# Linear attention of layer 0: the unread 2-byte matmuls inside its groups removed, the eight at its head kept

## The chip, the cores and the metric

One core of one Trainium2 chip runs the whole program. The metric is the device time of one execution in microseconds (us); lower is better. The engines are TensorE (PE in the profile, with its weight loads as PEld), VectorE (DVE), ScalarE (ACT), GpSimd (POOL) and the DMA queues.

## The reference

The program computes a small language-model tower: token embedding with neighbours, then four layers, each of an attention and a mixture of experts, on a stream h of 4 sequences x 512 tokens x 64 channels. The change touches only the first attention, which is linear attention with 8 heads of 32 key channels:

```
def _L0_attn_ref(x, Wks, Wqs, Wvs, Wo):
    keys = jnp.einsum('bsd,hdk->hbsk', x, Wks)
    queries = jnp.einsum('bsd,hdk->hbsk', x, Wqs)
    values = jnp.einsum('bsd,hde->hbse', x, Wvs)
    keys = jax.nn.elu(keys) + 1.0
    queries = jax.nn.elu(queries) + 1.0
    ...
    kv = jnp.einsum('hbsk,hbsd->hbsdk', keys, values)
    kv_cum = jnp.cumsum(kv, axis=2)
    numerator = jnp.einsum('hbsdk,hbsk->hbsd', kv_cum, queries)
    denominator = jnp.einsum('hbsk,hbsk->hbs', jnp.cumsum(keys, axis=2), queries)
    node = numerator / (denominator[..., None] + EPS)
    out = jnp.einsum('hbsd,hde->bse', node, Wo)
h = h + _L0_attn_ref(_layernorm(h, axis=-1), L0_attn_Wks, L0_attn_Wqs, L0_attn_Wvs, L0_attn_Wo)
```

## The kernel before

Everything is one program in stages, one after the other; the stage of this document is `linear_attention` (line 779), called once from `l0_attn` (line 2083) with G = 8 groups. A group g is four heads of one sequence (sequence g // 2, heads 4 * (g % 2) to 4 * (g % 2) + 3), and its two pairs of heads are p = 0 and 1. The 512 tokens of a sequence are cut into TB = 4 chunks of 128. Matrix operands are float32; one such matmul in the program stands as two in the trace.

For each group TensorE runs these steps, in this order (`diagonals` to `outs`, lines 841 to 899):

- `diagonals(g)`, L850: keys times queries inside each chunk, 16 matmuls over 32 rows each, into two banks per pair. VectorE then multiplies them by the causal mask into AT (L998, one instruction per pair, signal `masked`).
- `turn(g)`, L857: three transposes of key chunks. ScalarE copies them to KK (L942, `keys_ready`).
- `outs(g - 1, 0)` and `outs(g - 1, 1)`, L897: the result of the group before, CT, times the folded weights VO. VectorE divides by the denominator (L974, L976, L981, `heads_normed`) and GpSimd adds the heads to H (L1018).
- `state(g)`, L864: the running key-value sums. ScalarE copies them to SS (L944, `state_ready`).
- `within(g)`, L875: masked scores times values, 16 matmuls, into banks 6 and 7.
- `proj(g + 2)`, L838: keys and queries of the group after next. ScalarE takes them through Relu and Exp (L932, L935) and VectorE finishes them into QT and KT (L964, `qk_ready`).
- `across(g)`, L884: the sums of earlier chunks times the queries. ScalarE copies the result to CT (L949, `ctx_ready`).

Banks 0 to 5 of PSUM are three slots of two banks that go round over the steps in the order of `units`; before a step writes, `slot` waits until the step three places back has been read. By that rule `turn(g)` waits for `qk_ready` of group g + 1, and `outs(g - 1, p)` waits for `masked` of pair p of group g.

`unread(n, a)` (line 887) issues n matmuls of the bfloat16 identity, 128 x 128, on itself as 128 x 512, into bank a. Nothing reads what they write. They stand at three places: eight at the head of the stage (line 906); two in each `outs`, after `slot` and ahead of the wait for `ctx_ready` (line 893); and two in each group between `state` and `within` (line 916).

On VectorE a group also holds `draw` (L786, L788), work for a later stage. The queue of SyncE loads late weights in the first 8 us of the stage. The stage ends with a barrier of all engines.

Of the kernel before, what the change touches and what calls it, by code (L numbers as in the profile page):

```python
# [40 lines left out]
class Tally:  # L41
# [10 lines left out]
    def at(self, k):  # L52
        return self.i * self.per + (self.start + k) if self.per else self.start + k


def bc(ap, axis, n):

    shape = list(ap.shape)
    shape.insert(axis, n)
    return ap.unsqueeze(axis).to_broadcast(shape)  # L60
# [48 lines left out]
def _program(nc, T, out, ctx):  # L109
# [43 lines left out]
    C, a = {}, 0  # L153
# [625 lines left out]
    def linear_attention(G, batch, project, vo_src, vo_of, values, dst, eps):  # L779
# [39 lines left out]
        with nc.Block() as block:  # L819
# [6 lines left out]
            def _(eng):  # L826
                def slot(u):
                    n = number[u]
                    if n >= 3:
                        signal, value = freed(units[n - 3])  # L830
                        eng.wait_ge(signal.sem, value)
                    return bank(u)

                def proj(g):
                    a = slot(("P", g, 0))
                    for j in range(2):
                        for out, w, x in project(g, 0, j):
                            ins = nc.tensor.matmul(PS[out, a + j, :], w, x, start=True, stop=True, skip_group_check=True)  # L838
                    ins.then_inc(proj_done.sem, 1)

                def diagonals(g):
                    eng.wait_ge(qk_ready.sem, at(qk_ready, 2 * g + 1))
                    for p in range(2):
                        slot(("D", g, p))
                    for c in range(TB):
                        for p in range(2):
                            a = bank(("D", g, p))
                            for j in range(2):
                                h = rr(2 * p + j)
                                ins = nc.tensor.matmul(PS[:, a + j, chunk(c)], KT[h, g % 3, chunk(c)], QT[h, g % 3, chunk(c)], start=True, stop=True, skip_group_check=True)  # L850
                            if c == TB - 1:
                                ins.then_inc(diag_done.sem, 1)

                def turn(g):
                    a = slot(("T", g, 0))
                    for c in range(TB - 1):
                        ins = nc.tensor.transpose(PS[:, a, chunk(c)], KT[:, g % 3, chunk(c)], ident)  # L857
                    ins.then_inc(turned.sem, 1)

                def state(g):  # L860
                    a = bank(("T", g, 0)) + 1
                    eng.wait_ge(keys_ready.sem, at(keys_ready, g))
                    for c in range(TB - 1):
                        ins = nc.tensor.matmul(PS[:, a, c * D:(TB - 1) * D].rearrange("p (n d) -> p n d", d=D), KK[:, c, :], bc(XO[:, batch(g, 0) * TB + c, :], 1, TB - 1 - c),  # L864
                                               start=c == 0, stop=True, skip_group_check=True)
                    ins.then_inc(state_done.sem, 1)

                def within(g):
                    for p in range(2):
                        eng.wait_ge(masked.sem, at(masked, 2 * g + p))  # L870
                        if g >= 1:
                            eng.wait_ge(ctx_ready.sem, at(ctx_ready, 2 * (g - 1) + p))
                        for c in range(TB):
                            for j in range(2):
                                nc.tensor.matmul(PS[half(j), 6 + p, chunk(c)], XO[:, batch(g, j) * TB + c, :], AT[:, p, j, c, :],  # L875
                                                 start=c == 0, stop=c == 0, skip_group_check=True)

                def across(g):
                    eng.wait_ge(state_ready.sem, at(state_ready, g))
                    for p in range(2):  # L880
                        for c in range(1, TB):
                            for j in range(2):
                                h = rr(2 * p + j)
                                ins = nc.tensor.matmul(PS[half(j), 6 + p, chunk(c)], SS[h, c - 1, :], QT[h, g % 3, chunk(c)], start=False, stop=True, skip_group_check=True)  # L884
                        ins.then_inc(mixed.sem, 1)

                def unread(n, a):
                    for _ in range(n):
                        nc.tensor.matmul(PS[:, a, :], identh[:], bc(identh[:], 1, TB), start=True, stop=True, skip_group_check=True)

                def outs(g, p):
                    a = slot(("O", g, p))
                    unread(2, a)
                    eng.wait_ge(ctx_ready.sem, at(ctx_ready, 2 * g + p))
                    for c in range(TB):
                        for j in range(2):
                            ins = nc.tensor.matmul(PS[:, a + j, c * (D + 1):(c + 1) * (D + 1)], CT[half(j), p, chunk(c)], VO[half(j), vo_of(g, p), :],  # L897
                                                   start=True, stop=True, skip_group_check=True)
                    ins.then_inc(heads_out.sem, 1)
# [9 lines left out]
                for g in range(G):  # L909
                    diagonals(g)  # L910
                    turn(g)
                    if g >= 1:
                        outs(g - 1, 0)
                        outs(g - 1, 1)
                    state(g)
                    unread(2, 6)
                    within(g)
                    if g + 2 < G:
                        proj(g + 2)
                    across(g)  # L920
                outs(G - 1, 0)
                outs(G - 1, 1)

# [2129 lines left out]
```

## Time and profile before

| | us |
|---|---|
| median of 3 runs | 1049.62 (1047.46 to 1064.9) |
| profiled execution, its own time | 1049.9 |
| its span, first to last instruction | 1048.0 |
| mean granted clock of TensorE over the span | 0.925 of 2.4 GHz |
| the stage of the change, first `diagonals` to the last VectorE instruction | 122.9 to 221.7 |

Times within a trace count from the span's start. In a row of the page or of a view by lines, the engine, the line, the operation and out<-in stand first, then busy time or duration, and then the idle time of the engine just before with what ended it. The granted clock is 1.00 at 2.4 GHz and 0.50 at 1.2 GHz; TensorE has only these two levels in this trace, so a value between them is a mean over a stretch that has both. A row of busy time by stretches reads: the stretch A:B and its length, then the busy time of PE, PEld, DVE, ACT and POOL with the number of instructions, then TensorE's granted clock, the share of the DMA engines and GB/s.

### The profile page before, as it was taken

To read this page: it belongs to the slowest core of one execution; us is meant where nothing else is said; L and a number is where in the kernel's file an instruction comes from. 1 tells how busy PE (TensorE), PEld (TensorE's weight loads), DVE (VectorE), ACT (ScalarE), POOL (GpSimd) and SP (SyncE) were. 2 spreads that over 40 slices of the span, in tenths; PEclk is the share of its full clock that TensorE was granted. 3 is DMA by queue.
4 is the path that set the end of the run, shared out by engine and by line. 5 is a ranking of instruction groups with operands and counts; after the bars stand their busy time and mean duration, and the time that the engine had idled before them with its cause. 6 is when DMAs were issued, how large, how long until landed. Compare 5 with 4: busy or idle time off the path is not lost. (4 is left out here: it accounts for less than half of the span.)

```text
span 1048.0 us, 17078 instructions
## 1 busy us (share of the span) xinstructions
PE 904.0 (86%) x6611; PEld 454.4 (43%) x6611; DVE 649.8 (62%) x1734; ACT 368.5 (35%) x645; POOL 223.3 (21%) x291
## 2 busy tenths in 40 slices
PE   1988788979997865997898879999998799979998
PEld 0577566652323334762455333333333344443333
DVE  4977556567675264997467554555653555677665
ACT  0113533234543332223435314444444023443222
POOL 2600022215336031430230320121223402100000
PEclk9998899899999986998998968999999688989999
DMA  9300300000000001000000000000000000000000
GB/s 305 84 1 2 98 2 2 2 2 1 1 1 1 1 1 43 2 2 1 1 1 1 1 1 1 1 1 1 2 1 1 1 1 1 1 2 1 5 6 11
DMA packets 11477, 15.41 MB, mean 15 GB/s; under 512 B 8268, under 2 KB 9324, under 8 KB 10398
## 3 DMA queue, kind: packets, MB, share of 16 engines
q1 hardware_dynamic: 9976, 13.20, 4.2%
q10 hardware_dynamic: 1418, 1.09, 0.4%
q8 instruction: 54, 0.88, 0.4%
q14 instruction: 29, 0.24, 0.1%
HBM read 13.76 MB, written 0.52 MB: 14 GB/s over the span
## 5 line engine op out<-in xcount | busy, mean ns | idle before, releaser
L622 DVE TENSOR_REDUCE mx<-PS 128x2 f32<-128x1024 f32 (+3 forms) x104 | 109.6, 1095 | 103.8 <-PE PS L440 96.9
L582 ACT ACTIVATE arena<-PS 128x1024 f32<-128x1024 f32 (+3 forms) x104 | 91.0, 923 | 130.3 <-PE PS L470 130.3
L1217 DVE TENSOR_TENSOR arena<-arena,PS 128x512 f32<-128x512 f32 (+1 forms) x144 | 97.0, 684 | 45.0 <-ACT arena L1192 40.8
L1121 PE MATMUL PS<-XT,late 64*128 64x512 f32 (+1 forms) x288 | 101.9, 650 | 11.0 <-PEq L2502 6.6
L485 PE MATMUL PS<-arena 128*64 128x512 f32 (+3 forms) x416 | 99.8, 569 | 0.5 <-DVE arena L683 0.4
L465 PE MATMUL PS<-arena 32*128 32x512 f32 (+4 forms) x416 | 78.6, 622 | 9.7 <-ACT arena L559 7.4
L1192 ACT ACTIVATE arena<-PS,f_b_sb 128x512 f32<-128x512 f32 x96 | 61.8, 685 | 63.2 <-PE PS L1121 61.8
L1153 PE MATMUL PS<-arena,late 128*64 128x512 f32 (+1 forms) x288 | 81.6, 617 | 0.9 <-DVE arena L1217 0.7
L440 PE MATMUL PS<-arena 32*128 32x512 f32 (+4 forms) x416 | 72.8, 643 | 5.8 <-DVE arena L615 2.6
L1121 PEld LDWEIGHTS PS<-XT,late 64*128 64x128 f32 (+1 forms) x288 | 28.2, 183 | 62.5 <-ACT arena L1192 41.5
L1192 ACT ACTIVATE arena<-PS 114x512 f32<-114x512 f32 x48 | 27.4, 596 | 67.6 <-PE PS L1123 66.9
L1209 DVE TENSOR_TENSOR arena<-arena,PS 114x512 f32<-114x512 f32 x48 | 32.8, 683 | 28.8 <-ACT arena L1192 28.7
L727 POOL TENSOR_TENSOR H<-H,arena 128x256 f32<-128x256 f32 x30 | 21.8, 725 | 134.9 <-DVE arena L654 132.7
L465 PEld LDWEIGHTS PS<-arena 32*128 32x128 f32 (+1 forms) x416 | 29.9, 195 | 40.8 <-issue 18.5
L485 PEld LDWEIGHTS PS<-arena 128*64 128x64 f32 x416 | 22.1, 136 | 56.8 <-issue 38.9
L440 PEld LDWEIGHTS PS<-arena 32*128 32x128 f32 (+1 forms) x416 | 24.5, 203 | 49.6 <-issue 25.7
L2034 PE MATMUL PS<-identh 128*128 128x512 bf16 x91 | 31.6, 501 | 14.4 <-PEq L402 5.5
L1562 PE MATMUL PS<-late 128*128 128x128 fp8e5 x512 | 35.8, 235 | 7.2 <-DVE late L1471 7.2
L1123 PE MATMUL PS<-XT,late 64*114 64x512 f32 x96 | 40.6, 608 | 0.0
L1562 PEld LDWEIGHTS PS<-late 128*128 128x128 fp8e5 x512 | 33.1, 107 | 12.0 <-DVE late L1471 9.1
L2559 POOL TENSOR_TENSOR arena<-NB,vals 128x1280 f32<-128x1280 bf16 x11 | 25.7, 2338 | 57.6 <-DVE vals L2632 57.6
L1018 POOL TENSOR_TENSOR H<-H,arena 128x256 f32<-128x256 f32 x28 | 20.3, 725 | 76.6 <-DVE arena L981 74.6
(423 smaller groups left out, 1632.9 us busy)
## 6 DMA issues: line engine op xcount, KB each, us to landing
arena<-in_rel SPq DMA_DIRECT2D x4, 1024.0 KB, 11.8
late<-in_edges SPq DMA_DIRECT2D x2, 1024.0 KB, 11.4
late<-in_w_f_w SPq DMA_DIRECT2D x3, 342.0 KB
arena<-in_adj SPq DMA_DIRECT2D x1, 1024.0 KB, 6.7
late<-in_w_f_w SPq DMA_DIRECT2D x2, 512.0 KB, 3.7
Cc<-in_consts SPq DMA_DIRECT2D x1, 916.0 KB
arena<-in_ids ACTq DMA_DIRECT2D x1, 800.0 KB
late<-in_w_f_w SPq DMA_DIRECT2D x4, 128.0 KB, 3.8
```

Source lines behind the costliest of these rows:

```text
L440: ins = nc.tensor.matmul(PS[:, a + j, keys(c)], QT[h, g % 3, c * P:(c + 1) * P], KT[h, g % 3, keys(c)], start=True, stop=not causal, skip_ ...
L465: nc.tensor.matmul(PS[:, a + j, queries(c)], KT[h, g % 3, c * P:(c + 1) * P], QT[h, g % 3, queries(c)], start=True, stop=False, skip_group ...
L485: ins = nc.tensor.matmul(PS[half(j), 6 + p, queries(c)], XO[:, batch(g, j) * TB + c, :], PT[:, s % 2, p, j, queries(c)], start=c == 0, sto ...
L582: nc.scalar.activation(PT[:, s % 2, p, :, queries(c)], PS[:, a:a + 2, queries(c)], ACT.Exp, scale=scale).then_inc(exp_done.sem, 1)
L622: v.reduce_max(mx[:, g % 2, c, 2 * p:2 * p + 2], PS[:, a:a + 2, keys(c)], axis=AX.X).then_inc(max_done.sem, 1)
L1121: ins = nc.tensor.matmul(PS[0:rows, up_bank(n), :], w1(i)[r], XT2[r, b * S:(b + 1) * S], start=True, stop=True)
L1123: ins = nc.tensor.matmul(PS[0:rows, w3_bank(n), :], w3(i)[r], XT2[r, b * S:(b + 1) * S], start=True, stop=True)
L1153: nc.tensor.matmul(PS[half(i), out_bank(b), :], w2(i), HG[0:rows, n % 4, :], start=first, stop=i >= T - 2, skip_group_check=True).then_inc ...
L1192: nc.scalar.activation(HA[0:rows, n % 3, :], PS[0:rows, up_bank(n), :], act_fn, bias=bias).then_inc(hidden_done.sem, 1)
L1209: nc.vector.tensor_tensor(HM[0:rows, n % 2, :], ha, PS[0:rows, w3_bank(n), :], ALU.mult).then_inc(mixed_done.sem, 1)
L1217: nc.vector.tensor_tensor(HG[0:rows, n % 4, :], ha, PS[0:rows, gate_bank(n), :], ALU.mult).then_inc(gated_done.sem, 1)
L1562: ins = nc.tensor.matmul(PS[:, 6 + m % 2, n * P:(n + 1) * P], spelt[k % 3][:, g, P:2 * P], spelt[k % 3][:, g, 0:P], start=g % GROUP == 0, ...
```

## The change

The calls of `unread` inside the groups go: the two matmuls in each `outs` (16 calls, 32 matmuls) and the two between `state` and `within` (8 calls, 16 matmuls), 48 in all. The eight at the head stay. Nothing else differs; line numbers behind them move up by one or two, so that L897 reads L896 in the program after.

```diff
                 def outs(g, p):
                     a = slot(("O", g, p))
-                    unread(2, a)
                     eng.wait_ge(ctx_ready.sem, at(ctx_ready, 2 * g + p))
                     for c in range(TB):
                         for j in range(2):
...
                         outs(g - 1, 0)
                         outs(g - 1, 1)
                     state(g)
-                    unread(2, 6)
                     within(g)
                     if g + 2 < G:
                         proj(g + 2)
```

On TensorE's queue one group in the middle of the stage, from its `diagonals` (L850) to its `within` and `proj` (L875, L838), stood so before; PS is the PSUM tensor, arena the working memory in SBUF, identh the bfloat16 identity:

```order
L850 MATMUL PS<-arena 128x128 x16
L857 MATMUL PS<-Cc,arena 128x128 x3
L889 MATMUL PS<-identh 128x512 x2
L897 MATMUL PS<-arena 128x65 x8
L889 MATMUL PS<-identh 128x512 x2
L897 MATMUL PS<-arena 128x65 x8
L864 MATMUL PS<-arena 128x192
L864 MATMUL PS<-arena 128x128
L864 MATMUL PS<-arena 128x64
L889 MATMUL PS<-identh 128x512 x2
L875 MATMUL PS<-arena 64x128 x16
L838 MATMUL PS<-XT,a_wqk_sb 128x512 x2
```

The same group on TensorE's queue stands so now:

```order
L850 MATMUL PS<-arena 128x128 x16
L857 MATMUL PS<-Cc,arena 128x128 x3
L896 MATMUL PS<-arena 128x65 x16
L864 MATMUL PS<-arena 128x192
L864 MATMUL PS<-arena 128x128
L864 MATMUL PS<-arena 128x64
L875 MATMUL PS<-arena 64x128 x16
L838 MATMUL PS<-XT,a_wqk_sb 128x512 x2
L884 MATMUL PS<-arena 64x128 x12
```

The two `outs` of a group now follow each other and `turn`, and `within` follows `state`. The other engines' instructions and their order are the same in both programs.

## Rows read from the trace of the kernel before

**Rows 1.** The page: instructions in all, and granted clock in 40 slices of the span

```profile
span 1048.0 us, 17078 instructions
PEclk9998899899999986998998968999999688989999
```

**Rows 2.** One line's instructions: L889, ns min/median/max, and its waits

```profile
L889 PE MATMUL PS<-identh x56: 379/379/634, 119.1 to 217.7; 128*128 128x512 bf16 x56
  DVE arena L998: 10.3, 14
```

**Rows 3.** Busy time in stretches, first `diagonals` to next: groups 4, 5, 6

```profile
168.84:180.52 11.68, 10.26 (x142) 7.32 (x140) 7.53 (x18) 3.88 (x9) 2.90 (x4) 1.00 0.01 1
180.52:195.32 14.80, 13.38 (x141) 9.52 (x140) 7.53 (x18) 3.88 (x9) 2.90 (x4) 0.77 0.01 3
195.32:205.94 10.62, 9.20 (x137) 7.02 (x136) 7.53 (x18) 3.07 (x8) 2.90 (x4) 1.00 0.01 2
```

**Rows 4.** Timeline of PE: start, duration, instruction, idle before; groups 3 and 4

```profile
160.30 0.61 PE L889 MATMUL PS<-identh 128*128 128x512 bf16 x2 [0.58 <-DVE arena L998]
160.84 1.11 PE L897 MATMUL PS<-arena 64*128 64x65 f32 x16
161.88 0.60 PE L889 MATMUL PS<-identh 128*128 128x512 bf16 x2
162.41 1.11 PE L897 MATMUL PS<-arena 64*128 64x65 f32 x16
163.45 0.98 PE L864 MATMUL PS<-arena 128*128 128x192 f32 x6
164.27 0.59 PE L889 MATMUL PS<-identh 128*128 128x512 bf16 x2
164.80 1.97 PE L875 MATMUL PS<-arena 128*64 128x128 f32 x32
166.69 1.13 PE L838 MATMUL PS<-XT,a_wqk_sb 64*128 64x512 f32 x4
167.75 1.15 PE L884 MATMUL PS<-arena 32*64 32x128 f32 x24
168.84 1.17 PE L850 MATMUL PS<-arena 32*128 32x128 f32 x32
170.85 0.55 PE L857 MATMUL PS<-Cc,arena 128*128 128x128 f32 x3 [0.84 <-DVE arena L964]
```

**Rows 5.** Timeline of ACT and DVE behind `proj` of group 5, and DVE's masks

```profile
167.87 1.08 ACT L932 ACTIVATE arena<-PS 128x512 f32<-128x512 f32 x2 [3.08 <-PE PS L838]
168.84 1.15 ACT L935 ACTIVATE arena<-arena 128x512 f32<-128x512 f32 x2
...
169.50 1.29 DVE L964 SCALAR_TENSOR_TENSOR arena<-PS,arena 128x512 f32<-128x512 f32 x2 [2.91 <-ACT arena L935]
170.71 2.34 DVE L998 TENSOR_TENSOR arena<-PS,Cc 128x1024 f32<-128x1024 f32 x2
```

**Rows 6.** Timeline of PE in the first group, at the low clock

```profile
128.20 1.06 PE L889 MATMUL PS<-identh 128*128 128x512 bf16 x2
129.19 2.53 PE L875 MATMUL PS<-arena 128*64 128x128 f32 x32
```

**Rows 7.** Timeline at the stage's end: weights of the last `outs`, and DVE

```profile
216.44 0.97 PEld L897 LDWEIGHTS PS<-arena 64*128 64x128 f32 x16 [0.42 <-ACT arena L949]
...
219.63 0.16 DVE L974 TENSOR_SCALAR oden<-PS 128x8 f32<-128x8 f32 x1
```

**Rows 8.** Busy time in stretches around the falls of the clock, columns as in rows 3

```profile
181.60:185.00 3.40, 1.98 (x23) 1.23 (x21) 3.13 (x4) 1.51 (x4) 0.00 (x0) 1.00 0.00 0
185.00:191.80 6.80, 6.80 (x42) 4.89 (x42) 3.98 (x14) 0.32 (x1) 2.90 (x4) 0.50 0.00 1
...
123.50:130.40 6.90, 5.63 (x46) 4.10 (x41) 5.29 (x10) 1.63 (x4) 0.00 (x0) 0.51 0.41 107
157.70:161.10 3.40, 1.98 (x33) 1.12 (x27) 3.27 (x4) 2.05 (x5) 0.00 (x0) 1.00 0.02 5
```

## What the change will do to the time, worked out ahead of the run

> **What bounds the kernel now.** I read the page first. TensorE is the engine that nearly always has work, and its clock is not always granted in full: the row of tenths has many 8s and a few 6s, in all stages [rows 1]. So two things count here: TensorE's time in the stage, and its clock. Then I read the rows of L889, the matmuls that nobody reads: 56 of them, at the stage's head and in its groups, the last at 217.7 [rows 2]; eight of them stay and 48 go. TensorE sat idle ahead of them for L998 alone, 14 times (once for the weights and once for the matmuls, in seven groups). Nobody waits for their result, but they stand on TensorE's queue. Whether they cost time depends on whether they fill an idle gap or come behind it.
>
> The table of stretches answers how long a group is: from one `diagonals` to the next 11.68 us in a middle group, with 10.26 us of TensorE, 7.53 of VectorE and 3.88 of ScalarE [rows 3]. No engine is full, so the groups go by a loop over several engines, and the timelines show it. TensorE starts the first unread pair of group 3 at 160.30, after 0.58 us of waiting for L998, the mask. From there it runs without a gap to `proj` at 166.69 and on to `across` and `diagonals` of the next group [rows 4]. Behind `proj`, which is done at about 167.8, ScalarE runs Relu and Exp from 167.87, VectorE finishes the keys in L964 until 170.79, and only then does `turn` start at 170.85, after 0.84 us of idle TensorE. VectorE makes the first mask from 170.71 on, half of 2.34 us, and the next unread pair waits for that [rows 4, 5]. So the loop of a group is: mask, unread pair, `outs`, unread pair, `outs`, `state`, unread pair, `within`, `proj`, and then the chain of ScalarE and VectorE back to a mask. `across`, `diagonals` and `turn` run beside that chain, and so does all of TensorE's idle time in a group, 11.68 less 10.26 = 1.42 us. **All three unread pairs stand inside the loop, behind the wait and not in it.** They do not fill the idle gap.
>
> **The price of the instructions.** From group 3 [rows 4]: the first pair holds TensorE from 160.30 to 160.84, 0.54 us; the second from 161.88 to 162.41, 0.53; the third from 164.27 to 164.80, 0.53. Its weights must be loaded too and `state` ends in a short matmul, so for the third I take 0.6. Without the first pair `outs` starts at 160.30 and ends at 161.34. The second `outs` waits for the second mask, which VectorE has ready 2.34 us after the first one began; in group 3 that is 161.37 (the row of group 4, 170.71 plus 2.34, less 11.68), and with the 0.06 us from a VectorE end to a TensorE start (170.79 to 170.85) it starts at 161.43, where it started at 162.41. So 0.98 us of the two pairs' 1.07 are gained, and 0.09 turns into a wait. With the third pair a group gains 1.58 us, and would take 10.10 at the full clock. Groups 1 to 7 have all three: 7 x 1.58 = 11.1. The first group has only the third pair, at the low clock: 128.20 to 129.19, 0.99 us [rows 6]. Behind the last group the first `outs` waits for ScalarE's copy anyway, until 216.44, and the end is VectorE's, which is busy with the first pair of heads until 219.63 while the second is long ready [rows 7]; those two pairs give nothing. Sum: 12.1 us.
>
> What might eat it on other engines: VectorE's 7.53 us and POOL's 2.90 per group fit in 10.10, and the copies that `within`, `proj` and `across` wait for follow steps that move with them. No DMA is issued in the groups that hold the unread matmuls except late weights, which a later stage reads.
>
> **The price of the clock.** In this stage the clock was at 1.2 GHz twice, from 123.5 to 130.4 and from 185.0 to 191.8 [rows 8]. What TensorE did before the second fall is the thin part of a group: it finished `diagonals`, idled, did three transposes, idled again, and started an unread pair and `outs`; 1.98 us busy in 3.40. In group 3 the same part, cut at 157.70, was as busy, 1.98 us, and the clock stayed [rows 8]. So before the change this part lies at the edge, and in groups 1 to 7 it fell once. What the fall cost stands in the table: group 5 took 14.80 us, 3.12 more than group 4, with a mean clock of 0.77 [rows 3]; everything from `outs` to the middle of `within` ran at half speed (the pair and `within` in rows 6 show the same: 1.06 and 2.53 us, for 0.59 and 1.97 in rows 4).
>
> The change thins just this part. The unread matmuls are the only ones there that fill all 128 rows with 512 columns on end; in their place comes `outs`, 64 rows and 65 columns, whose matmuls start 65 ns apart (16 in 1.04 us), and `state`. The idle 1.42 us stay, in a shorter group. I therefore expect the clock to fall in most groups: not in one of seven but in five or six, since the part is now thinner in every group alike, and only chance in where it lies keeps it from falling each time. The trace cannot show the share; it can only bound it, between none and all seven. I take 5.5.
>
> Here a rule of the notes bears on the case: the Trainium skill, "TensorE: Matmul & The Clock Gate", section "A second HAM failure mode: psum-queue depth-cycling", says that a TensorE that idles briefly and often between groups of matmuls, as it goes round PSUM banks, makes its clock swing between the two levels. The trace agrees so far as the idle gaps of a group are waits of `slot` for a bank and a fall came once behind them; how much more often it falls without the filler no row shows.
>
> **The sum.** The profiled execution took 1049.9 us, 0.3 more than the median. Less 12.1 it is 1037.8, with one fall in groups 1 to 7 as before. With n falls it is 1037.8 + 3.12 x (n - 1): 1034.7 for none, 1047.2 for four, 1050.3 for five, 1053.4 for six, 1056.5 for all seven. With 5.5 it is 1051.8; I say 1052. The change would give back in clock what it takes in instructions.
>
> **The rivals.** *The clock stays up*: three falls or fewer, 1034.7 to 1044. For it speaks that equally busy parts of groups 1 to 4, 6 and 7 passed without a fall, and that TensorE is never idle for more than 0.84 us at a time in a middle group. Against it, that the part before 185.0 fell even with the pairs in it. The same page, section "HAM oscillation — how this bites in real kernels", has a rule by which only a long idle gap between bursts takes the clock down; by it this rival would win, with the time of none or one fall, 1034.7 to 1037.8. The fall at 185.0 behind gaps of 0.84 and 0.58 us speaks against that rule, so it gets little.
>
> *The low clock lasts longer*: this is the one that ends slower. At the low clock the part after a fall is thinner than before, since its unread pairs are gone (they took 0.99 us each time in rows 6). If the clock then stays down for half as long again, 10.2 in place of 6.8 us, a fall costs half as much again, 4.7 us, and seven falls give 1034.7 + 32.8 = 1067.5. It decides against the change from three falls on: 12.1 gained plus the 3.1 of before's own fall, 15.2, are used up by 15.2 / 4.7 = 3.2 falls (at the price of 3.12, by 4.9).
>
> *The gain turns into waits*: if the masks, or the chain behind `proj`, came later by as much as TensorE comes earlier, nothing would change, 1049.9. The chain starts from `proj` itself and moves with it, and the second mask costs only 0.09 us, so this is unlikely.
>
> **How the numbers follow.** Four to seven falls at about 3.1 us, 1047 to 1057: 0.62. Three or fewer, 1034 to 1045: 0.20. The longer low clock, 1057 to 1071: 0.14. Waits in place of the gain, 1050: 0.04. The rest of the program has its own falls [rows 1], which shift when this stage ends earlier or later; the three runs of one and the same kernel lie 17 us apart, so I allow some us to both sides. The range 1041 to 1061 leaves about 1 in 10 below and 1 in 10 above. Two per cent is 21 us, about what a measurement of this kernel can tell from no change: faster means under 1028.6, below even the case of no fall, 0.01; slower means over 1070.6, the far end of the second rival, 0.04; within, 0.95.
>
> **What the profile after will show.** Right, if: `outs` starts at once behind the first mask and its second half some 0.1 us behind the first half; `within` follows `state` with no gap; a group at 2.4 GHz takes 10.1 us from `diagonals` to `diagonals`, and one with a fall about 13.2; the mean clock from 133 to 215 is well under the 0.96 or so of before, with five or six low stretches, each beginning near the first `outs` of a group; VectorE's and ScalarE's durations are the same. Wrong, if the clock is up in four or more of the seven groups, if a low stretch spans a whole group, or if groups at the full clock take more than 10.3 us.

## The result and the profile after

The kernel after takes 1066.56 us in the median of 20 runs (1058.39 to 1071.69), the kernel before 1053.95 in the median of 20 (1047.46 to 1068.51): a ratio of 1.0116, with a 95% interval from 1.0085 to 1.0147. **The change makes the kernel slower, by 12.6 us in these medians; forecast was 1052, 2 us slower, in a range that ended at 1061.** A later set of runs of the same two kernels (`after_third` below) has 7.2 us between the medians, ratio 1.0056, interval 1.0009 to 1.0103: both sets show that the kernel after is slower, and their intervals together leave from 1 to 15 us. The profiled execution of after took 1070.52 us, its span is 1068.6, and the mean granted clock over it is 0.894, where before had 0.925.

The page of the kernel after, and the rows of its line L889 (answering to [rows 1] and [rows 2]):

```profile
span 1068.6 us, 16998 instructions
PEclk9869877788999986996988887999999788999999
L889 PE MATMUL PS<-identh x8: 379/379/390, 123.7 to 125.2; 128*128 128x512 bf16 x8
```

Eight unread matmuls are left, at the head. In slices 6 to 8 of the clock stand three 7s, where before had one 8 among 9s: that is the stage of the change. Busy time by stretches, from one `diagonals` to the next, for groups 1 to 6 of the kernel after ([rows 3] has groups 4 to 6 of before):

```profile
137.92:151.16 13.24, 11.81 (x136) 10.05 (x134) 7.54 (x18) 3.88 (x9) 2.89 (x4) 0.74 0.01 1
151.16:164.58 13.42, 11.97 (x135) 10.07 (x133) 7.54 (x18) 3.87 (x9) 2.89 (x4) 0.75 0.01 2
164.58:178.07 13.49, 12.04 (x136) 10.00 (x134) 7.54 (x18) 3.88 (x9) 2.89 (x4) 0.75 0.00 1
178.07:191.51 13.44, 12.00 (x136) 9.93 (x134) 7.54 (x18) 3.88 (x9) 2.89 (x4) 0.75 0.00 1
191.51:204.96 13.45, 12.00 (x136) 9.86 (x134) 7.54 (x18) 3.88 (x9) 2.90 (x4) 0.75 0.01 2
204.96:215.73 10.77, 9.32 (x131) 8.18 (x129) 7.54 (x18) 3.07 (x8) 2.90 (x4) 0.84 0.01 2
```

Every one of these groups has a fall, and the last one only a short one. The mean clock in a group is 0.74 to 0.75 and in the last 0.84, where a group of before at the full clock took 11.68 us. The last group, from 215.73 to the stage's end at 231.70, has a mean clock of 0.85 in the trace, so a short fall stands there too; before had 1.00 in that part. VectorE and ScalarE are unchanged. The timeline of PE in group 2 of the kernel after (answering to [rows 4]) and the stretches before and in its low clock (answering to [rows 8]):

```profile
153.17 0.55 PE L857 MATMUL PS<-Cc,arena 128*128 128x128 f32 x3 [0.84 <-DVE arena L962]
154.30 3.10 PE L896 MATMUL PS<-arena 64*128 64x65 f32 x32 [0.58 <-DVE arena L996]
157.33 1.75 PE L864 MATMUL PS<-arena 128*128 128x192 f32 x6
159.02 3.50 PE L875 MATMUL PS<-arena 128*64 128x128 f32 x32
162.44 1.13 PE L838 MATMUL PS<-XT,a_wqk_sb 64*128 64x512 f32 x4
```

```profile
151.90:155.30 3.40, 1.98 (x35) 1.52 (x30) 3.40 (x4) 1.85 (x4) 0.00 (x0) 1.00 0.00 0
155.40:162.20 6.80, 6.78 (x54) 6.53 (x54) 3.99 (x14) 0.32 (x1) 2.89 (x4) 0.50 0.02 4
```

The idle gaps are where and as long as they were, 0.84 and 0.58 us. TensorE is busy for 1.98 of the 3.40 us ahead of the fall, as in the two stretches of before, of which one was followed by a fall and one was not; what it is busy with is different.

The stage, from the first `diagonals` to the last VectorE instruction, took 98.80 us before (122.93 to 221.73) and 104.15 after (127.55 to 231.70). So 5.4 of the 20.6 us between the two profiles lie in it. The rest shows when the execution is cut at the same VectorE instructions in each kernel: up to the first attention; that attention and the entry of its experts; the experts and attention up to the graph; the graph's sums; the experts and norms of layers 1 and 2; the rest. The first three of these stretches and the fifth, for the kernel before, the kernel after, and a further profile of the kernel after (`after_third` below), columns as in rows 3:

```profile
0.00:113.00 113.00, 79.98 (x746) 59.19 (x748) 83.59 (x259) 26.20 (x62) 26.26 (x25) 0.94 0.30 91
113.00:232.50 119.50, 102.12 (x1279) 72.31 (x1275) 70.43 (x183) 42.22 (x86) 21.46 (x30) 0.93 0.08 23
232.50:411.20 178.70, 148.09 (x819) 56.31 (x817) 103.96 (x302) 70.81 (x115) 57.60 (x88) 0.90 0.02 7
485.20:647.80 162.60, 142.87 (x899) 68.39 (x898) 94.69 (x262) 64.84 (x117) 30.02 (x51) 0.88 0.00 1
```

```profile
0.00:117.60 117.60, 84.29 (x746) 64.18 (x748) 83.50 (x258) 26.08 (x62) 26.07 (x25) 0.88 0.29 88
117.60:242.50 124.90, 107.09 (x1231) 86.23 (x1229) 70.60 (x183) 42.34 (x86) 21.42 (x30) 0.78 0.07 22
242.50:423.20 180.70, 146.91 (x820) 56.55 (x819) 104.07 (x302) 71.01 (x115) 57.62 (x88) 0.91 0.02 7
497.20:669.40 172.20, 154.32 (x900) 71.88 (x898) 94.73 (x263) 65.23 (x117) 30.00 (x51) 0.82 0.00 1
```

```profile
0.00:111.90 111.90, 80.90 (x746) 60.91 (x748) 83.46 (x259) 26.10 (x62) 26.00 (x25) 0.92 0.30 92
111.90:237.10 125.20, 107.05 (x1231) 86.40 (x1227) 70.45 (x183) 42.31 (x86) 21.44 (x30) 0.78 0.08 22
237.10:418.20 181.10, 147.24 (x820) 56.63 (x819) 103.99 (x302) 71.03 (x115) 57.60 (x88) 0.91 0.02 7
492.20:654.10 161.90, 142.31 (x900) 68.49 (x898) 94.70 (x262) 65.07 (x117) 30.01 (x51) 0.89 0.00 1
```

The second row, which holds the changed stage, is the same in both profiles of after, 125 us at a clock of 0.78. The others are code that the change does not touch. The first and the last have two courses or more, that is, lengths that the same code takes in different executions: 112 to 113 or 117.6 us ahead of the stage, 162 or 172 in the experts behind the graph (167.9 in `before_again`), and the long ones have the low clocks, 0.88 and 0.82. One and the same kernel after took 1070.5 and 1052.7 us so.

The third row is 2.0 and 2.4 us longer after, and there another difference stands, which is not one of TensorE's clock. Ahead of the graph's sums all engines stand idle, and their queues hold only the register and branch instructions of a loop and a barrier. Before and after, the first matmuls behind it with TensorE's idle time, and the row of one branch of its queue from the view of that line, duration in ns:

```profile
401.77 0.37 PE L2516 MATMUL PS<-identh,NB 128*128 128x128 bf16 x2 [4.83 <-PEq L2387]
L2234 PEldq COMPARE_BRANCH  x1: 370/370/370, 400.8 to 400.8; - x1
```

```profile
413.74 0.37 PE L2514 MATMUL PS<-identh,NB 128*128 128x128 bf16 x2 [7.80 <-PEq L2385]
L2232 PEldq COMPARE_BRANCH  x1: 3172/3172/3172, 410.0 to 410.0; - x1
```

One and the same branch took 0.37 us before and 3.17 after, and the barrier behind it, at which every engine waits, came as much later. It is no chance of one execution: it took 2.62 to 3.41 us in all four profiles of the kernel after that reach it, whole or cut short, and 0.36 to 0.46 us in all nine of the kernel before, of its delayed version and of the versions with filler. The two programs differ in nothing but the 48 matmuls that are gone from TensorE's queue ahead of this branch; how that makes the branch slow no run shows.

### The profile page after: what moved, and what is told of

Same layout as the page of the kernel before. It is cut to its first block and busy times, and to the rows that moved or that the text cites. A ratio compares the mean times of both kernels' runs of the same rounds, so it can differ in the third digit from the quotient of the medians.

```text
span 1068.6 us, 16998 instructions
## 1 busy us (share of the span) xinstructions
PE 920.6 (86%) x6563; PEld 475.4 (44%) x6563; DVE 650.4 (61%) x1734; ACT 369.0 (35%) x645; POOL 223.1 (21%) x291
## 5 line engine op out<-in xcount | busy, mean ns | idle before, releaser
L1119 PE MATMUL PS<-XT,late 64*128 64x512 f32 (+1 forms) x288 | 106.3, 675 | 11.4 <-PEq L2500 6.6
L1560 PEld LDWEIGHTS PS<-late 128*128 128x128 fp8e5 x512 | 34.9, 111 | 12.1 <-DVE late L1469 9.1
```

Of the source, the lines that this page charges most:

```text
L1119: ins = nc.tensor.matmul(PS[0:rows, up_bank(n), :], w1(i)[r], XT2[r, b * S:(b + 1) * S], start=True, stop=True)
L1560: ins = nc.tensor.matmul(PS[:, 6 + m % 2, n * P:(n + 1) * P], spelt[k % 3][:, g, P:2 * P], spelt[k % 3][:, g, 0:P], start=g % GROUP == 0, ...
```

## The experiments

All of them change TensorE's filler, add a delay, or end the program early. The times of before beside them were measured together with them.

### Where the filler stands, and what it fills

The kernel after, with one pair per group, 16 unread matmuls in all, put into the idle gap behind `turn`, into the bank that `state` writes next:

```diff
                     diagonals(g)
                     turn(g)
+                    unread(2, bank(("T", g, 0)) + 1)
                     if g >= 1:
```

> The kernel after, with two unread matmuls per group put right behind `turn`, ahead of the wait for the first mask, so that they lie in TensorE's 0.58 us of idle time and not behind it. Theory (the clock falls because the part between `diagonals` and `within` is too thin): the part is fuller than in the kernel before as well, so the low stretches of groups 1 to 7 go, seven in the kernel after and one in the profile before; a group takes about 10.1 us from `diagonals` to `diagonals`, and the time is 1034 to 1043 us, faster than both. Rival (any filler is only time, and the falls have another cause, such as where the stage lies in the execution): falls in most groups as after, 1060 to 1070 us. Rival (idle gaps for a bank make the clock fall, whatever stands between them): the gap ahead of `turn` of 0.84 us stays, so falls stay in most groups.

Measured: 1045.63 us in the median (1039.17 to 1050.60, 6 runs), before 1055.22, ratio 0.9888 (0.9826 to 0.9949). Timeline of PE in one group of this kernel, and the group's stretch:

```profile
150.44 0.55 PE L857 MATMUL PS<-Cc,arena 128*128 128x128 f32 x3 [0.84 <-DVE arena L963]
150.82 0.59 PE L889 MATMUL PS<-identh 128*128 128x512 bf16 x2
151.57 2.24 PE L896 MATMUL PS<-arena 64*128 64x65 f32 x32 [0.15 <-DVE arena L997]
153.74 0.98 PE L864 MATMUL PS<-arena 128*128 128x192 f32 x6
154.66 1.97 PE L875 MATMUL PS<-arena 128*64 128x128 f32 x32
```

```profile
138.16:148.43 10.27, 9.26 (x138) 7.19 (x136) 7.54 (x18) 3.88 (x9) 2.90 (x4) 1.00 0.01 2
```

The pair shortens the second gap from 0.58 to 0.15 us and delays nothing. No group from 1 to 6 has a fall (each takes 10.26 or 10.27 us, group 6, which has no `proj`, 9.21), and the stage takes 85.48 us, 13 less than before. The median lies 2.6 us over my upper expectation, and between two kinds of runs: three took 1039 to 1041 us, as expected, and three 1050 to 1051. The profile is of one of the second kind, and has the longer courses ahead of the stage and behind the graph.

The kernel before, with the 48 matmuls made small: 32 rows and 32 columns of the array, as many columns moved.

```diff
+                def thin(n, a):
+                    for _ in range(n):
+                        nc.tensor.matmul(PS[0:32, a, :], identh[0:32, 0:32], bc(identh[0:32, :], 1, TB), start=True, stop=True, skip_group_check=True)
...
-                    unread(2, a)
+                    thin(2, a)
...
-                    unread(2, 6)
+                    thin(2, 6)
```

> The kernel before, but each of the 48 unread matmuls in the groups uses 32 rows and 32 columns of the array in place of 128 and 128, with the same 512 columns moved and so the same time on TensorE. Theory (what the clock wants is how much of the array works): falls in all seven groups as after, and nothing is gained in instructions: a group at the full clock takes 11.7 us, and the time is that of the kernel after plus up to 12.1 us, 1066 to 1080 us. Rival (TensorE's busy time alone counts): the clock does as before, one to three falls in groups 1 to 7, and the time is that of the kernel before, 1047 to 1060 us.

Measured: 1084.28 us (1081.74 to 1091.25, 6 runs), before 1055.22, ratio 1.0262 (1.0210 to 1.0314). Timeline of PE and two groups of this kernel:

```profile
159.66 0.60 PE L893 MATMUL PS<-identh 32*32 32x512 bf16 x2 [0.58 <-DVE arena L1002]
161.23 0.60 PE L893 MATMUL PS<-identh 32*32 32x512 bf16 x2
```

```profile
140.01:156.51 16.50, 15.07 (x141) 10.64 (x139) 7.54 (x18) 3.88 (x9) 2.90 (x4) 0.69 0.00 1
156.51:171.47 14.96, 13.54 (x142) 10.01 (x140) 7.54 (x18) 3.88 (x9) 2.89 (x4) 0.77 0.01 2
```

At the full clock the pairs take their 0.60 us as the full ones do, so TensorE is as busy, and yet each of the groups 1 to 6 of this profile has a fall (14.95 to 16.53 us). This is the run that decides between the theory and its rival: with the same time on TensorE at the same places, pairs on the whole array let the clock fall in one of these groups (two in `before_again` below) and pairs on 32 rows and 32 columns in all six. Whether it is the rows, the columns or the data moved that count, the run doesn't tell apart. The stage took 126.46 us (127.41 to 253.87), since the falls come on top of the full length of the queue; the median is 4 us over the expected range.

### One kind of pair alone

Only the call of `unread` in `outs` removed:

```diff
                     a = slot(("O", g, p))
-                    unread(2, a)
```

> Only the pairs in `outs` removed; the pair between `state` and `within` stays. Theory (the pairs behind `turn` hold the clock): 7 x 0.98 = 6.9 us gained in instructions, a group at the full clock takes about 10.7 us, falls in five to seven of groups 1 to 7, and the time is about that of the kernel after, 1055 to 1070 us. Rival (each pair counts alike): fewer falls than after, three to four, and a time between the two kernels' or under both, 1045 to 1055 us.

Measured: 1061.25 us (1049.13 to 1070.56, 12 runs), before 1055.22, ratio 1.0045 (1.0001 to 1.0089). Groups 2 and 4 of its profile, from an execution of 1049.3 us:

```profile
144.63:155.33 10.70, 9.25 (x137) 7.09 (x136) 7.54 (x18) 3.88 (x9) 2.91 (x4) 1.00 0.01 2
166.03:178.35 12.32, 10.87 (x138) 8.30 (x136) 7.54 (x18) 3.89 (x9) 2.89 (x4) 0.86 0.01 1
```

The group at the full clock is 10.70 us, as worked out. But in this execution groups 1 to 6 had one short fall only, where five to seven were expected, and the part behind `turn` is as thin here as in the kernel after. The execution is one of the two shortest of the 12; how many falls the others had, no profile shows.

Only the call between `state` and `within` removed:

```diff
                     state(g)
-                    unread(2, 6)
                     within(g)
```

> Only the pair between `state` and `within` removed; the pairs in `outs` stay. Theory: the thin part behind `turn` is as before, so one or two falls in groups 1 to 7; 0.99 + 7 x 0.6 = 5.2 us gained, a group at the full clock takes about 11.1 us, and the time is 1043 to 1053 us, some 4 to 5 us under the kernel before. Rival (each pair counts alike): two to three falls more than before, which take the gain back: 1050 to 1060 us.

Measured: 1052.42 us (1042.79 to 1061.96, 12 runs), before 1055.22, ratio 0.9961 (0.9921 to 1.0001). Groups 2 and 4 of its profile:

```profile
144.71:155.96 11.25, 9.83 (x139) 7.25 (x137) 7.54 (x18) 3.88 (x9) 2.91 (x4) 1.00 0.01 2
167.21:181.58 14.37, 12.95 (x139) 9.81 (x137) 7.54 (x18) 3.88 (x9) 2.90 (x4) 0.76 0.01 1
```

One fall, as before; a group gains 11.68 less 11.25 = 0.43 us. The third pair is not worth the 0.6 that I gave it. The median lies in the expected range, but the interval takes in 1, so a gain over the kernel before isn't shown.

### The same kernels once more, and a delay

The kernels after and before without any edit, for more profiles:

> The kernel after, once more, for a second profile. Theory: the stage of the change is the same in every execution, 104 us from the first `diagonals` to its last VectorE instruction with seven falls in groups 1 to 7, and what differs from run to run is elsewhere: the stretch ahead of the stage (112.2 or 116.8 us in the profiles so far) and the experts and norms behind the graph (from VectorE's instruction 980 of 1734 to 1240, 162.6 or 172 us). Rival: the number of falls in the stage differs too, and with it the stage's time.

> The kernel before, once more, for a second profile. Theory: the stage takes 98.8 us with one fall in groups 1 to 7, or up to two falls and 3 us more; the two places named for the kernel after have one of the same two times each. Rival: the stage of the kernel before takes over 104 us in such a run, so that the change costs nothing there and all of the difference comes from elsewhere.

> The kernel after, timed beside the two with a delay, and a third profile of it. Theory: 1058 to 1071 us, median near 1066; four or more falls in groups 1 to 7. Rival (chance in the 20 runs before): a median under 1062.

`after_again` took 1065.72 us, `before_again` 1054.52; `after_third` 1066.10 in the median (1052.73 to 1069.44, 10 runs) with 1058.93 for before, ratio 1.0056 (1.0009 to 1.0103). The median of `after_third` is as expected, but three of its ten runs took 1052.7 to 1055.1. The stage took 98.66 us in `after_again`, 104.50 in `after_third`, 103.90 in `before_again`. So both my expectations were too simple: the stage is not the same in every execution of either kernel. Over all profiles that hold the unchanged stage of either kernel, with those of the next two parts, it took 98.8 to 99.1 us in four of the five of before and 103.9 in the fifth, and 104.2 to 104.5 in six of the eight of after, 102.9 and 98.7 in the others. The last groups of `after_again` and four groups of `before_again`:

```profile
178.57:190.40 11.83, 10.38 (x135) 8.47 (x133) 7.54 (x18) 3.88 (x9) 2.90 (x4) 0.86 0.01 1
190.40:200.67 10.27, 8.82 (x136) 7.02 (x134) 7.54 (x18) 3.89 (x9) 2.90 (x4) 1.00 0.01 2
200.67:209.88 9.21, 7.76 (x132) 6.72 (x130) 7.54 (x18) 3.08 (x8) 2.91 (x4) 1.00 0.01 2
```

```profile
144.07:155.76 11.69, 10.26 (x142) 7.32 (x140) 7.54 (x18) 3.89 (x9) 2.91 (x4) 1.00 0.01 2
155.76:170.57 14.81, 13.38 (x142) 9.52 (x140) 7.54 (x18) 3.88 (x9) 2.91 (x4) 0.77 0.00 1
170.57:186.98 16.41, 14.98 (x141) 10.71 (x140) 7.54 (x18) 3.88 (x9) 2.90 (x4) 0.69 0.00 1
186.98:198.66 11.68, 10.25 (x141) 7.32 (x139) 7.54 (x18) 3.88 (x9) 2.90 (x4) 1.00 0.01 4
```

The kernel after can pass two groups without a fall; the kernel before can have two in a row, and one can cost 4.73 us.

Three kernels tested whether the course of the experts behind the graph is set by the moment at which they start. The edit is the same in all, with n memsets of an unread tile; by the profiles of the kernel before, n = 3 delays by 2.3 us:

```diff
         graph_lists()
+        later(n)
         graph_sums()
```

> The kernel after, with three memsets of an unread tile on VectorE and a barrier ahead of the graph's sums, behind the stage of the change: some 2 to 3 us of pure delay. Theory (the changed stage ends at another moment against the clock's own, and so hits the slow one of two courses in the experts behind the graph, 172 us in place of 162.6): the delay moves it to the fast course, and the kernel is faster than after in spite of the delay, 1056 to 1063 us in the median. Rival (the slow course has nothing to do with when the experts start): the median is that of after plus the delay, 1068 to 1071 us.

> The same delay in the kernel before. Theory: it moves those runs that took the fast course in the experts behind the graph to the slow one or leaves a mixture; the median is above before plus the delay, 1058 to 1066 us. Rival: before plus the delay, 1055 to 1058 us.

> The kernel after with one memset and a barrier ahead of the graph's sums, about 1.3 us of delay in place of 2.3. Theory (the moment at which the experts behind the graph start decides their course): a part of the runs takes the fast course there; median 1058 to 1066 us. Rival (delay is only delay): median of the kernel after plus 1.3 us, 1067 to 1069 us.

> The kernel after with eight memsets and a barrier there, about 4.8 us of delay. Theory: again a part of the runs takes the fast course, and the median is 1062 to 1068 us, less than after plus 4.8. Rival (delay is only delay): 1070 to 1073 us.

Medians: the kernel after with n = 3, 1062.39 us (ratio to before 1.0088, 1.0043 to 1.0132); before with n = 3, 1056.13 (1.0031, 0.9998 to 1.0064); after with n = 1, 1063.23 (1.0030, 0.9986 to 1.0075); after with n = 8, 1071.62 (1.0111, 1.0031 to 1.0191, 4 runs). The theory had named the first and the third of them, and missed `before_shift`, which came out at its rival's value, and `after_shift_long`, whose rival had 1070 to 1073. But the intervals of the first and the third overlap that of the plain kernel after measured later (1.0009 to 1.0103). And the delay changed something else: in the profile with n = 3 the long branch of TensorE's queue took 0.43 us (2.66 with n = 1, 2.55 with n = 8), and from the last VectorE instruction ahead of the delay to ScalarE's first behind it 6.45 us passed, for 7.04 in the plain kernel after (6.43 and 4.08 in the two kernels before). So there the n = 3 kernel was not delayed against the plain one at all, and some 2.5 us of its lower median are the branch's. `after` and `after_third` took 172.2 and 161.9 us in the experts and began them 5.0 us apart, which would fit the theory, but a pair of profiles can't show it. So that the moment decides the course is neither shown nor ruled out.

### The program cut short

Two pairs of kernels end early and write H there: behind the first attention (cut0: all experts and later layers are left out), and behind the experts of layer 1 (cut1: layers 2 and 3 are left out).

```diff
     l0_attn()
-    to_attn = Entering([...])
-    l0_ffn(to_attn)
...
+    stored()
```

> The kernel before, ended behind the first attention: everything from the first experts on is left out and H is written instead. It is one side of a pair with after_cut0. In the profile before the stage's last VectorE instruction ends at 221.7 us; with the store 226 to 232 us in the median, and a spread of 10 us or so.

> The kernel after, ended in the same place (the rest left out, H written). Theory (the stage itself loses a little, the rest of the difference is elsewhere): 2 to 5 us more than before_cut0 in the median. Rival (all of the difference is the stage's own, in executions that no profile showed): 8 to 12 us more. Rival (the stage is a wash): within 1.5 us.

> The kernel before, ended behind the experts of layer 1 (layers 2 and 3 are left out, and H is written). One side of a pair with after_cut1; by the profile before about 535 to 550 us.

> The kernel after, ended in the same place (layers 2 and 3 left out, H written). Theory (the later stages take the slower of their courses more often behind the changed stage): the difference to before_cut1 is larger than that of the first pair by 2 to 6 us. Rival (what differs outside the stage is chance of the few runs): the difference is that of the first pair, within 1.5 us.

Medians: 228.51 before and 235.55 after for cut0 (6 runs each, means 229.8 and 235.1); 527.12 and 531.70 for cut1 (6 and 5 runs, means 525.8 and 531.0). At the end of the changed stage the difference is 7.0 us by the medians, above the 2 to 5 expected, and 5.3 by the means. The 7.0 belong to no pair of executions. Of the six before four took 227.9 to 228.6 us and two 232.7 and 232.9; of the six after one took 229.2, two 232.3 and 232.7, and three 238.4 to 239.3. In the profiles of all the kernels the stage begins either at 121.2 to 123.2 us or at 127.2 to 127.8, and the shorter and the longer times lie about as far apart; of the longer kind no profile was taken here. Like with like, and the 229.2 left aside, after is 4.2 us longer (232.5 less 228.3) or 5.9 (238.7 less 232.8), around the 5.4 of the two profiles of the stage.

At the end of layer 1 the difference is 4.6 and 5.2 us, as the rival said. These runs lie 13 us apart, so they can't tell 2 or 3 us: the profile of `after_cut1` has the long branch too (2.62 us for 0.37), and the stage takes 104.24 us in it for 99.07, together more than the means show. `before_cut1` came out 8 us under its expected range. The whole program shows 12.6 us by the medians of the first 20 runs and 7.2 by those of the later ones. The stage and the branch make 8.2; whether the rest of the 12.6 arises further on or is chance stays open.

### A version that beats both

```diff
-                unread(8, 6)
+                unread(16, 6)
...
                     turn(g)
+                    unread(2, bank(("T", g, 0)) + 1)
...
                 outs(G - 1, 0)
                 outs(G - 1, 1)
+                unread(12, 6)
```

> The version with two unread matmuls behind each `turn`, and two places more where TensorE idles: 16 in place of 8 at the stage's head, ahead of the first wait of 1.97 us, and 12 behind the last `outs`, while VectorE finishes. Theory: they fill gaps and cost nothing; the low stretch near the first group and the one around the stage's end go, 1 to 4 us less than the version with the filler behind `turn` alone, 1036 to 1048 us in the median. Rival (the course of later stages decides, and it is chance): the median is that of the other version or above, 1045 to 1052 us.

Measured: 1045.35 us (1041.19 to 1050.30, 6 runs), before 1058.93, ratio 0.9892 (0.9835 to 0.9949). The first group takes 8.33 us in place of 10.54, and there is no low clock in the whole stage, which takes 83.25 us. Against before it is as good as the pair behind `turn` alone (0.9888), and the median fits the theory's range and the rival's; whether the two further places are worth the 2.2 us of the stage these runs can't tell.

## Why the prediction was wrong

**The loop and the pairs' place: right.** The pairs stood behind the wait. Without them `outs` starts at the first mask (0.58 us of idle time, as before), and no new wait came up.

**The price of the instructions: 12.1 forecast, 10.4 measured.** A group at the full clock takes 10.27 us (`after_again`, `fill_gap`) and not 10.10. In `after_again` both `outs` take 2.17 us (193.55 to 195.72) where they took 3.15 with their pairs: 0.98, as forecast. The term that was off is the third pair, 0.43 to 0.44 in place of 0.6, 1.1 us over seven groups; and the first group gave 0.50 (10.87 less 10.37) in place of 0.99. So it is 7 x 1.41 + 0.50 = 10.4.

**The price of a fall: right.** 13.45 less 10.27 is 3.18 us, for 3.12 forecast.

**The number of falls: 5.5 forecast, worth of about six in the profile.** It has a full one in each of groups 1 to 5 and short ones in group 6 (10.77 - 9.21 = 1.56 us) and behind it. In groups 1 to 6 the other two profiles of the whole kernel have three full and one short (`after_again`) and five full and one short (`after_third`, where group 6 took 12.17 us). The stage came out 5.4 us longer in the first pair of profiles and 5.3 in the means of cut0, where 1.9 was forecast. Of the 3.4 us between 5.35 and 1.94, the instructions make 1.7 (10.4 for 12.1) and the falls the other 1.7: they cost 15.7 us, 5.35 + 10.4, beyond before's own, where 4.5 x 3.12 = 14.0 was forecast. That before has one fall was itself the count of one profile; `before_again` has two, one of them longer.

**What makes the clock fall: right in the kind, open in the place.** That the clock would give back what the instructions save is shown by `thin_filler` and `fill_gap`. The prediction put it to the part from `diagonals` to `outs`. `fill_gap` fills that part and ends the falls, but `keep_state_pair` leaves it as thin as in the kernel after and had one short fall in its profile. So it is not shown that this part alone decides.

**The sum's base and all that lies outside the stage: this is the step that failed.** "The profiled execution took 1049.9 us, 0.3 more than the median": that was a median of three. Over 20 runs the kernel before takes 1053.95, 4.1 us more. Its profiled execution had short courses ahead of the stage and behind the graph, and I added the stage's difference to them as if they were the kernel's. The rest of the program was put at nothing but "some us to both sides". Its branch ahead of the graph's sums alone adds 3.17 less 0.37 = 2.8 us, always to the same side; and the same kernel after ran in 1052.7 and in 1071.7 us, mostly by parts outside the change. With the 3.4 us that the stage was off the sum is 1051.8 + 4.1 + 3.4 + 2.8 = 1062.1, past the range's end at 1061. The 4.5 us from there to 1066.6 no experiment has placed. They may be chance of the first set of runs, since in the later set the whole difference is 7.2 us, less than the stage's 5.4 and the branch's 2.8 together; that stays open.

**The rivals.** *The clock stays up* fell: no profile of after shows it, and `after_again` comes nearest, with three full falls and a short one in groups 1 to 6. With it falls, as the only cause, the rule of the Trainium skill, "TensorE: Matmul & The Clock Gate", section "HAM oscillation — how this bites in real kernels", that a long idle gap is what takes the clock down: here it fell in group after group with no gap over 0.84 us. The section "A second HAM failure mode: psum-queue depth-cycling" agrees with these rows, but by itself it would not tell the kernel after from `fill_gap`, which has the same waits for banks and no falls. *The low clock lasts longer* came out in `thin_filler` (16.50 us) and in `before_again` (16.41), not in the kernel after; the 1067 us that this rival gave are where the median came to lie, but not for its reason. *Waits in place of the gain*: none.

## What to carry to other kernels

A matmul that nobody reads can be worth its time, and an order to remove it has to be priced with the clock: here 48 of them cost 10.4 us of the stage, and without them the falls cost 15.7 us more. Put such filler in front of a wait, where TensorE idles anyway, and not behind it, and use the whole array: one pair per group in the gap behind `turn` made the kernel 1.1% faster than before and about 2% faster than without any (0.9888 against 1.0116, or 1.0056 in the later runs; 2.8 us of that is the branch), while one pair per group behind `state` came out at 1.0045. A base for a sum should be a median of many runs, or a profile whose other stages have been compared with a second one. And where a change takes instructions away, look in the profile after for idle time in code that did not change.

## What the runs showed of the hardware

TensorE's busy time alone did not tell whether its clock would fall: 1.98 us busy of 3.40 stood ahead of a fall and ahead of none. Pairs of 32 x 32 in place of 128 x 128, as long and at the same places, took the kernel from 1055 to 1084 us, with a fall in each of six groups, where the kernel before had one or two. This program on one core has a spread of 20 us in 1055, and the long executions have the lower mean clocks: a stretch of unchanged code took 162 us with a mean clock of 0.88 or 0.89, and 172 with 0.82. And a branch of TensorE's queue, in code that did not change, took 2.6 to 3.4 us in each of four profiles of the kernel after and 0.4 in each of four of the kernel before, and no engine had work meanwhile.
